# A GpSimd clear ahead of each position gather and each hop gather or scatter, and a smaller one ahead of each window gather

## The chip, the core and the metric

The kernel runs on one core of a Trainium2 chip. The metric is device microseconds of one execution, from its first to its last instruction on that core with what the device adds around it. The engines are TensorE (PE; PEld are its weight loads), VectorE (DVE), ScalarE (ACT), GpSimd (POOL) and SyncE (SP), which only issues DMAs. GpSimd issues the indirect DMAs: gathers and scatters of one row per partition, 128 rows each, whose row numbers stand in SBUF.

## The reference

Four graph layers run one after the other on 100,000 nodes of 32 features and 25,000 edges sorted by destination, each followed by a residual sum and a normalisation:

```python
x = _layernorm(x + _L0_gnn_ref(x, edge_weight, edge_attr_3, edge_index, ...), axis=-1)
x = _layernorm(x + _L1_gnn_ref(x, edge_index), axis=-1)
x = _layernorm(x + _L2_gnn_ref(x, edge_index, edge_attr_32, ...), axis=-1)
x = _layernorm(x + _L3_gnn_ref(x, edge_attr3_2x32, src, dst, ...), axis=-1)
```

- L0: each edge's weight goes through a small network (1 to 64 to 384); the result is contracted with the edge's direction and the source's features, and the messages are added up by destination.
- L1: three hops of a normalised sum over edges: `msgs = norm[:, None] * x[src]; x = segment_sum(msgs, dst)`, added up and divided by 4.
- L2: a network on both ends' features and the edge's own, then the maximum by destination.
- L3: attention over two heads: scores, a softmax by destination, messages, their sum by destination, and a last product with `W1`.

## The kernel before

A node that is no edge's destination takes a short path: its result depends on its own row alone. The kernel works with that. Edges lie in SBUF as 128 partitions of T = 196 columns; a chunk is 28 columns, so there are 7. Tables in DRAM hold one row per edge position, and an edge finds the latest value of its source there.

The stages in order of time, as the trace shows them:

1. *Histogram and positions* (to 196 us). One-hot products on PE count destinations; a table of positions, `pos_table`, is stored. POOL gathers the first source and destination rows and then, for 56 columns, each source's position (`pos_x`, named `out_short<-pos_table` in the trace; line 777). DVE meanwhile computes directions and folds weights (lines 1708 to 1760). These are many small instructions.
2. *Edge products of L0* (196 to 650 us). ACT makes the hidden layer (line 975), PE multiplies (L1310), DVE contracts. POOL gathers the other sources from `x_pos`, which needs all chunks of `x` copied and stored, then the destinations. The last 84 destination columns have a clear ahead of each gather (`gather_dst`, line 785).
3. *Hops of L1, with all nodes' short path beside them* (770 to 1204 us). POOL takes 60 columns by `short_columns` and writes them out again (lines 822 to 856), and takes and writes 22 columns by `second_columns`. Between these, PE, ACT and DVE work on 14 chunks of nodes in four lots, `nodes(...)`: PE turns rows (`n_turned`) and multiplies, ACT copies what was turned (line 1006) and takes the products, DVE normalises. The first of DVE's instructions of each half chunk is a reduction of `work`.
4. *Edge network of L2* (1243 to 1530 us). POOL gathers 7 windows of 16 columns into `work`, with a clear of `nodes_w` ahead of each gather. DVE waits for a window at line 2253 (`move_window`) and PE and ACT follow it.
5. *Attention of L3* (1530 to 1731 us and beyond). The same with windows into `A_msg`.
6. *Final scatters* (1731 to 2041 us). 196 of them, in order of readiness, line 880.

What sets the order around the change: each engine's program is written by hand, and engines meet at semaphores. POOL's queue is strictly in order. Within `gather`, `keep()` makes POOL wait for DVE now and then, so that it doesn't run too far ahead. Within `short_columns`, `keep(t)` makes it wait for a node chunk. A clear with its own semaphore `cleared`, and POOL's wait for it, stands between one indirect DMA and the next where `cleared_tile` is given: the DMA isn't begun until the clear has ended. The tile cleared is of no use at that time: `gtmp[0:HF]` is 64 by 64 words, `nodes_w` 128 partitions of 256 words.

Of the kernel before, what the change touches and what calls it, by code (L numbers as in the profile page):

```python
# [21 lines left out]
HEADS, HF = 2, 64  # L22
# [16 lines left out]
SLOTS_IN_WINDOW = 16  # L39
# [9 lines left out]
GATHER_CHUNK = 28  # L49
# [13 lines left out]
def parts_until(k):  # L63
    return sum(TABLE_PARTS[:k + 1])
# [24 lines left out]
def gnn_kernel(nc, x, src, dst, r_feat, rel, turned_attr, edge_weight, w1, b1, w2, b2,  # L89
# [12 lines left out]
    with ExitStack() as ctx:  # L102
        def sb(name, shape, dt=f32):
            return ctx.enter_context(nc.sbuf_tensor(name, shape, dt))

        def sem(name):
            return ctx.enter_context(nc.semaphore(name))
# [107 lines left out]
        gtmp = sb("gtmp", [HF + 1, HF])  # L215
# [6 lines left out]
        nodes_w = sb("nodes_w", [P, 2 * P])  # L222
# [51 lines left out]
        cleared = sem("cleared")  # L274
# [422 lines left out]
        def _(pool):  # L697
# [32 lines left out]

            node_limit, edge_limit = pool.to_reg(N_NODES - 1), pool.to_reg(E_PAD - 1)

            def gather(column, of, idx, limit, done, columns=range(T), keep=None, cleared_tile=None):

                for t in columns:
                    if keep:
                        keep()
                    if cleared_tile is not None:
                        issued["cleared"] += 1
                        pool.memset(cleared_tile, 0.0).then_inc(cleared, 1)  # L740
                        pool.wait_ge(cleared, issued["cleared"])
                    pool.indirect_dma_start(  # L742
                        out=column(t), out_offset=None, in_=of,
                        in_offset=bass.IndirectOffsetOnAxis(ap=idx[:, t:t + 1], axis=0),
                        bounds_check=limit, oob_is_err=False).then_inc(done(t), 16)
# [3 lines left out]
            issued = {"hist": 0, "radial": 0, "cleared": 0}  # L749
# [15 lines left out]
            def gather_dst(columns, keep, cleared_tile=None):  # L765
# [6 lines left out]
                   keep=keep_to_histogram)  # L772
# [2 lines left out]
            gather_dst(range(DST_FIRST * GATHER_CHUNK), keep_to_histogram)  # L775
            pool.wait_ge(pos_stored, 32)
            gather(lambda t: pos_x[:, t:t + 1], pos_table, src_i, node_limit, lambda t: pos_rows, range(plain),
                   keep=keep_to_radial)

            for k in range(XP_SLOTS):  # L780
                pool.wait_ge(x_stored[k], 16 * len(range(k, D_CHUNKS + 1, XP_SLOTS)))
# [11 lines left out]
            def short_columns(move, done, columns, keep=None):  # L793

                for t in columns:
                    if keep and keep(t):
                        pool.wait_ge(n_out, keep(t))
                    move(t).then_inc(done, 16)
                if columns.stop < FEWEST:
                    return  # L800
                turns["short"] += 1
                with pool.If(n > FEWEST):
                    for t in range(FEWEST, FEW):
                        move(t).then_inc(more_done, 16)
                    pool.wait_ge(more_done, 16 * (FEW - FEWEST) * turns["short"])
                with pool.If(n > FEW):
                    pool.wait_ge(msg_cleared, 1)
                    for t in range(FEW, T):
                        move(t).then_inc(rest_done, 16)
                    pool.wait_ge(rest_done, 16 * (T - FEW) * turns["short"])  # L810
                pool.sem_inc(short_in, 1)

            def second_columns(move):

                turns["second"] += 1
                for t in range(FEWEST2):
                    move(t).then_inc(hop_done, 16)
                with pool.If(n2 > FEWEST2):
                    for t in range(FEWEST2, T):
                        move(t).then_inc(hop_rest, 16)  # L820
                    pool.wait_ge(hop_rest, 16 * (T - FEWEST2) * turns["second"])
                pool.sem_inc(short_in, 1)
# [7 lines left out]
            def put_short(of, idx, column):  # L830
# [7 lines left out]
                          keep=lambda t: max(t - 24, 0) // 15)  # L838
# [20 lines left out]
            for k, of, order in zip((3, 4), compact, WINDOW_ORDER):  # L859

                pool.wait_ge(table_stored, 16 * parts_until(k))
                pool.wait_ge(gather_ok, k + 2)

                with pool.If(n > FEW):
                    for c in range(CHUNKS):
                        gather(lambda t: of[:, t, :], tables[k], pos_i, edge_limit, lambda t: wide_rows,
                               range(c * GATHER_CHUNK + SLOTS_IN_WINDOW, (c + 1) * GATHER_CHUNK))
                    pool.wait_ge(wide_rows, 16 * CHUNKS * (GATHER_CHUNK - SLOTS_IN_WINDOW) * (k - 2))
                pool.sem_inc(wide_in, 1)
                for i, c in enumerate(order):  # L870
                    here = window_rows[k - 3][i % SLOTS]
                    if i >= SLOTS:
                        pool.wait_ge(here, 16 * SLOTS_IN_WINDOW * (i // SLOTS))
                    gather(lambda t: of[:, t, :], tables[k], pos_i, edge_limit, lambda t: here,
                           range(c * GATHER_CHUNK, c * GATHER_CHUNK + SLOTS_IN_WINDOW), cleared_tile=nodes_w[:])

            for i, c in enumerate(LAST_ORDER):
                pool.wait_ge(final_ready, i + 1)
# [1731 lines left out]
```

## Time and profile before

| | us |
|---|---|
| three timed runs | 2048.66, 2029.43, 2053.27; median 2048.66 |
| the profiled execution's own time | 2061.06 |
| its span, first to last instruction | 2059.3 |
| busy: PE, PEld, DVE, ACT, POOL | 796.0, 595.5, 1345.8, 486.9, 1284.9 |

No engine is busy for more than two thirds of the span, so the time is made of stretches with different limits. To read it, one takes the chain of waits for the shares, then a timeline of each engine where the chain names something odd. A wait is written after the instruction that waited, as [us <-releaser]. "remote", or in the chain "another core or an unknown queue", stands where no work in the trace released it; "issue" stands where the engine waited for nothing that the trace shows. Both may be long.

### The profile page before, as it was taken

To read this page: it belongs to the slowest core of one execution; us is meant where nothing else is said; L and a number is where in the kernel's file an instruction comes from. 1 tells how busy PE (TensorE), PEld (TensorE's weight loads), DVE (VectorE), ACT (ScalarE), POOL (GpSimd) and SP (SyncE) were. 2 spreads that over 40 slices of the span, in tenths; PEclk is the share of its full clock that TensorE was granted. 3 is DMA by queue.
4 is the path that set the end of the run, shared out by engine and by line. 5 is a ranking of instruction groups with operands and counts; after the bars stand their busy time and mean duration, and the time that the engine had idled before them with its cause. 6 is when DMAs were issued, how large, how long until landed. Compare 5 with 4: busy or idle time off the path is not lost.

```text
span 2059.3 us, 14157 instructions
## 1 busy us (share of the span) xinstructions
PE 796.0 (39%) x3676; PEld 595.5 (29%) x3676; DVE 1345.8 (65%) x2600; ACT 486.9 (24%) x1014; POOL 1284.9 (62%) x1393
## 2 busy tenths in 40 slices
PE   7801545541333003616313500155621757265122
PEld 3300222220111003515313400145521657265112
DVE  9942959896958970784605496167684899397610
ACT  7721311110100121423202320033320334143200
POOL 8875576674478857515871207888128888637775
PEclk9955866786765555866756755566765776565555
DMA  8072511110110211222201412000000111010000
GB/s 313 16 240 89 201 26 29 27 30 15 20 17 12 76 43 32 100 77 87 89 6 68 158 74 98 4 8 19 18 29 12 32 28 29 18 28 22 10 12 8
DMA packets 64092, 114.25 MB, mean 55 GB/s; under 512 B 27599, under 2 KB 48648, under 8 KB 63224
## 3 DMA queue, kind: packets, MB, share of 16 engines
q1 hardware_dynamic: 24304, 80.96, 10.9%
q0 software_dynamic: 33728, 12.79, 4.5%
q10 hardware_dynamic: 5960, 19.43, 2.5%
q8 instruction: 31, 0.51, 0.1%
q14 instruction: 69, 0.57, 0.1%
HBM read 61.66 MB, written 55.21 MB: 57 GB/s over the span
## 4 chain that ended last, share of the span: by engine, by line
DVE 36%; issue 21%; POOL 20%; PE 12%; another core or an unknown queue 6%; ACT 4%; DMA 1%; DVEq 0%; ACTq 0%; POOLq 0%; PEld 0%; PEldq 0%
DVE work L1484 12%; POOL A_dst L742 8%; POOL work L742 7%; DVE work L1495 5%; PE bank L1261 4%; PE bank L1235 3%; POOL nodes_w L740 2%; POOL A_msg L742 2%; PE bank L1348 2%; DVE A_dst L1484 2%; DVE A_tmp L1484 1%; DVE r L1495 1%; DVE small L1495 1%; PE bank L1421 1%
## 5 line engine op out<-in xcount | busy, mean ns | idle before, releaser
L1495 DVE TENSOR_REDUCE work<-work 128x80 f32<-128x1280 f32 (+3 forms) x147 | 204.5, 1420 | 186.8 <-ACT work L1016 148.9
L742 POOL DMA_INDIRECT A_dst<-in_x,dst_i x196 | 223.4, 1140 | 108.7 <-DVE work L1495 48.7
L1310 PE MATMUL bank<-w2fold,work 128*128 128x384 f32 x392 | 200.6, 658 | 232.4 <-DVE work L1484 136.4
L880 POOL DMA_INDIRECT out<-A_dst,out_i x196 | 211.5, 1079 | 99.0 <-issue 61.7
L1484 DVE TENSOR_TENSOR work<-bank,work 128x384 f32<-128x384 f32 (+1 forms) x294 | 154.6, 589 | 80.3 <-remote 43.1
L1348 PE MATMUL bank<-nodes_w,small 128*128 128x128 f32 (+1 forms) x784 | 137.1, 341 | 162.0 <-ACT small L1006 95.6
L742 POOL DMA_INDIRECT A_src<-x_pos,A_tmp x140 | 145.0, 1036 | 73.1 <-issue 41.8
L1310 PEld LDWEIGHTS bank<-w2fold,work 128*128 128x128 f32 x392 | 91.0, 251 | 340.8 <-issue 310.0
L740 POOL MEMSET nodes_w<- 128x256 f32 x224 | 73.0, 326 | 168.4 <-DMA table<-A_dst 168.2
L1348 PEld LDWEIGHTS bank<-nodes_w,small 128*128 128x128 f32 (+1 forms) x784 | 125.9, 249 | 172.9 <-ACT small L1006 104.6
L742 POOL DMA_INDIRECT work<-table,pos_i x112 | 142.0, 1268 | 30.9 <-POOL nodes_w L740 30.9
L1235 PE MATMUL bank<-ident,work 128*128 128x128 f32 (+1 forms) x294 | 67.9, 346 | 235.7 <-DVE work L1484 134.8
L975 ACT ACTIVATE work<-A_tmp,b1col,w1col 65x256 f32<-65x256 f32 x98 | 58.4, 599 | 415.3 <-PE bank L1310 184.4
L742 POOL DMA_INDIRECT A_msg<-table,pos_i x112 | 132.3, 1182 | 32.2 <-POOL nodes_w L740 30.6
L1235 PEld LDWEIGHTS bank<-ident,work 128*128 128x128 f32 (+1 forms) x294 | 45.7, 185 | 240.2 <-issue 127.5
L1235 PE MATMUL bank<-ident,end_col 128*32 128x128 f32 (+2 forms) x18 | 6.8, 379 | 259.6 <-DVE end_col L1540 230.9
L831 POOL DMA_INDIRECT edge_sums<-A_sum,out_short x60 | 66.2, 1104 | 60.1 <-DVE A_sum L1484 42.2
L1235 PE MATMUL bank<-ident,A_tmp 128*65 128x128 f32 (+1 forms) x203 | 45.4, 366 | 150.6 <-DVE A_tmp L2369 144.1
L825 POOL DMA_INDIRECT A_msg<-table,nxt_i x60 | 66.5, 1108 | 55.8 <-DVE work L1484 20.2
L742 POOL DMA_INDIRECT A_src<-in_x,A_tmp x56 | 73.3, 1309 | 16.9 <-issue 16.9
L1261 PE MATMUL bank<-A_msg,A_sum 128*128 128x392 f16 x392 | 80.0, 340 | 1.7 <-ACT A_sum L929 1.7
L1421 PE MATMUL bank<-gw,A_tmp 128*128 128x128 f32 x392 | 76.7, 361 | 8.3 <-issue 5.7
(397 smaller groups left out, 2306.8 us busy)
## 6 DMA issues: line engine op xcount, KB each, us to landing
work<-in_x SPq DMA_DIRECT2D x26, 960.0 KB
x_pos<-A_sum SPq DMA_DIRECT2D x13, 990.0 KB
out<-work ACTq DMA_DIRECT2D x13, 960.0 KB
A_tmp<-ew_turned_rows ACTq DMA_DIRECT2D x49, 130.0 KB
table<-A_dst SPq DMA_DIRECT2D x2, 3136.0 KB
edge_sums<-A_dst SPq DMA_DIRECT2D x2, 3136.0 KB
table<-A_dst SPq DMA_DIRECT2D x13, 448.0 KB
A_tmp<-in_edge_attr_2x SPq DMA_DIRECT2D x49, 112.0 KB
```

The costliest lines, as they stand in the source:

```text
L740: pool.memset(cleared_tile, 0.0).then_inc(cleared, 1)
L742: pool.indirect_dma_start(out=column(t), out_offset=None, in_=of, in_offset=bass.IndirectOffsetOnAxis(ap=idx[:, t:t + 1], axis=0), bounds_ ...
L825: return lambda t: pool.indirect_dma_start(out=column(t), out_offset=None, in_=of, in_offset=bass.IndirectOffsetOnAxis(ap=idx[:, t:t + 1], ...
L831: return lambda t: pool.indirect_dma_start(out=of, out_offset=bass.IndirectOffsetOnAxis(ap=idx[:, t:t + 1], axis=0), in_=column(t), in_off ...
L880: pool.indirect_dma_start(out=out, out_offset=bass.IndirectOffsetOnAxis(ap=out_i[:, t:t + 1], axis=0), in_=A_dst[:, t, :], in_offset=None, ...
L1235: return nc.tensor.transpose(out_ap, in_ap, ident[0:n, 0:n])
L1261: last = nc.tensor.matmul(banks[6 + h][:, 0:half], lo_hot[:, 2 * slot + j, :], hi_hot[:, 2 * slot + j, h * half:(h + 1) * half], start=Fal ...
L1310: last = nc.tensor.matmul(banks[2 * (u % PAIRS_DEEP) + j][:, 0:PATHS], hid_rows[:, u % PAIRS_DEEP, j * P:(j + 1) * P], w2_rows[:], start=T ...
L1348: last = nc.tensor.matmul(node_products(i, w)[0:parts, k * P:(k + 1) * P], n_xT[:, s, k * parts:(k + 1) * parts], nodes_w[:, w * P:(w + 1) ...
L1421: last = nc.tensor.matmul(banks[2 + slot][:, j * P:(j + 1) * P], cat3_rows[:, slot, j * P:(j + 1) * P], gw2_rows[:], start=True, stop=True)
L1484: return v.tensor_tensor(out=o, in0=a, in1=b, op=op)
L1495: return v.tensor_reduce(out=o, in_=a, axis=AX, op=op)
```

## The change

The clear and its wait become a function, `pause`. It is called now in three more places: ahead of each of the 56 position gathers, ahead of each column of `short_columns` (60 gathers, 60 scatters in four pieces) and of `second_columns` (22 columns, three times). These are 242 clears of `gtmp[0:HF]` more. The 224 clears ahead of the window gathers are now of `gtmp[0:HF]` too, not of `nodes_w`. Inside the branches that these inputs don't take nothing is added.

```diff
--- before.py
+++ after.py
@@ -730,15 +730,19 @@
 
             node_limit, edge_limit = pool.to_reg(N_NODES - 1), pool.to_reg(E_PAD - 1)
 
+            def pause(tile):
+
+                issued["cleared"] += 1
+                pool.memset(tile, 0.0).then_inc(cleared, 1)
+                pool.wait_ge(cleared, issued["cleared"])
+
             def gather(column, of, idx, limit, done, columns=range(T), keep=None, cleared_tile=None):
 
                 for t in columns:
                     if keep:
                         keep()
                     if cleared_tile is not None:
-                        issued["cleared"] += 1
-                        pool.memset(cleared_tile, 0.0).then_inc(cleared, 1)
-                        pool.wait_ge(cleared, issued["cleared"])
+                        pause(cleared_tile)
                     pool.indirect_dma_start(
                         out=column(t), out_offset=None, in_=of,
                         in_offset=bass.IndirectOffsetOnAxis(ap=idx[:, t:t + 1], axis=0),
@@ -775,7 +779,7 @@
             gather_dst(range(DST_FIRST * GATHER_CHUNK), keep_to_histogram)
             pool.wait_ge(pos_stored, 32)
             gather(lambda t: pos_x[:, t:t + 1], pos_table, src_i, node_limit, lambda t: pos_rows, range(plain),
-                   keep=keep_to_radial)
+                   keep=keep_to_radial, cleared_tile=gtmp[0:HF])
 
             for k in range(XP_SLOTS):
                 pool.wait_ge(x_stored[k], 16 * len(range(k, D_CHUNKS + 1, XP_SLOTS)))
@@ -795,6 +799,7 @@
                 for t in columns:
                     if keep and keep(t):
                         pool.wait_ge(n_out, keep(t))
+                    pause(gtmp[0:HF])
                     move(t).then_inc(done, 16)
                 if columns.stop < FEWEST:
                     return
@@ -814,6 +819,7 @@
 
                 turns["second"] += 1
                 for t in range(FEWEST2):
+                    pause(gtmp[0:HF])
                     move(t).then_inc(hop_done, 16)
                 with pool.If(n2 > FEWEST2):
                     for t in range(FEWEST2, T):
@@ -872,7 +878,7 @@
                     if i >= SLOTS:
                         pool.wait_ge(here, 16 * SLOTS_IN_WINDOW * (i // SLOTS))
                     gather(lambda t: of[:, t, :], tables[k], pos_i, edge_limit, lambda t: here,
-                           range(c * GATHER_CHUNK, c * GATHER_CHUNK + SLOTS_IN_WINDOW), cleared_tile=nodes_w[:])
+                           range(c * GATHER_CHUNK, c * GATHER_CHUNK + SLOTS_IN_WINDOW), cleared_tile=gtmp[0:HF])
 
             for i, c in enumerate(LAST_ORDER):
                 pool.wait_ge(final_ready, i + 1)
```

On POOL, at the position gathers (`out_short` holds `pos_x`), before:

```order
L729 MEMSET work 128x768
L742 DMA A_src<-in_x,A_tmp 128x32 x56
L742 DMA A_dst<-in_x,dst_i 128x32 x28
L742 DMA out_short<-pos_table,A_tmp 128x1 x56
L742 DMA A_src<-x_pos,A_tmp 128x33 x140
```

and now:

```order
L729 MEMSET work 128x768
L746 DMA A_src<-in_x,A_tmp 128x32 x56
L746 DMA A_dst<-in_x,dst_i 128x32 x28
L736 MEMSET gtmp 64x64
L746 DMA out_short<-pos_table,A_tmp 128x1
```

The 56 gathers, which stood in one row, now alternate with a clear each, and the last two rows of the second piece repeat 56 times.

On POOL, at the first hop's gathers (`A_msg` from the first table), before:

```order
L790 TENSOR_LOAD n_short
L790 ISA x2
L825 DMA A_msg<-table,nxt_i 128x33 x60
L802 COMPARE_AND_BRANCH
L825 DMA A_msg<-table,nxt_i 128x33 x4
```

and now:

```order
L746 DMA A_dst<-in_x,dst_i 128x32
L794 TENSOR_LOAD n_short
L794 ISA x2
L736 MEMSET gtmp 64x64
L831 DMA A_msg<-table,nxt_i 128x33
```

Here too a clear stands ahead of each of the 60 gathers; the loads of the counts and the branches are where they were. The scatters and the later hops' gathers are changed in the same way.

On POOL, at the start of the first edge network's windows, before:

```order
L864 COMPARE_AND_BRANCH
L742 DMA work<-table,pos_i 128x32 x84
L864 UNCONDITIONAL_BRANCH
L740 MEMSET nodes_w 128x256
L742 DMA work<-table,pos_i 128x32
```

and now:

```order
L870 COMPARE_AND_BRANCH
L746 DMA work<-table,pos_i 128x32 x84
L870 UNCONDITIONAL_BRANCH
L736 MEMSET gtmp 64x64
L746 DMA work<-table,pos_i 128x32
```

The 84 gathers of the first row belong to the branch that isn't taken. Nothing moved; the clear is of a smaller tile.

## Rows read from the trace of the kernel before

**Rows 1.** The page: the span, and its section 4, the chain that ended last.
```profile
span 2059.3 us, 14157 instructions
...
DVE 36%; issue 21%; POOL 20%; PE 12%; another core or an unknown queue 6%; ACT 4%; DMA 1%; DVEq 0%; ACTq 0%; POOLq 0%; PEld 0%; PEldq 0%
```

**Rows 2.** Timeline of POOL, three places: start us, us, engine, line, operation [idle before <-releaser].
```profile
480.55 1.00 POOL L742 DMA_INDIRECT A_dst<-in_x,dst_i  x1 [0.30 <-issue]
...
677.56 0.17 POOL L740 MEMSET gtmp<- 64x64 f32 x1
678.00 1.00 POOL L742 DMA_INDIRECT A_dst<-in_x,dst_i  x1 [0.27 <-POOL gtmp L740]
...
1640.23 0.33 POOL L740 MEMSET nodes_w<- 128x256 f32 x1
1640.82 1.05 POOL L742 DMA_INDIRECT A_msg<-table,pos_i  x1 [0.27 <-POOL nodes_w L740]
```

**Rows 3.** Waits, whole span: engine line <- releaser: us in total, times, longest us.
```profile
ACT small L1006 <- remote: 121.1, 9, 31.8
```

**Rows 4.** Timeline, hops (770 to 1204 us), by engine: ACT, PE, POOL, DVE.
```profile
794.75 0.48 ACT L1006 COPY small<-bank 128x384 f32<-128x384 f32 x1 [9.43 <-remote]
...
820.82 0.48 ACT L1006 COPY small<-bank 128x384 f32<-128x384 f32 x1 [24.82 <-remote]
...
1071.72 0.48 ACT L1006 COPY small<-bank 128x384 f32<-128x384 f32 x1 [31.76 <-remote]
...
1041.98 0.85 PE L1235 MATMUL bank<-ident,work 128*128 128x128 f32 x3
...
841.40 0.99 POOL L825 DMA_INDIRECT A_msg<-table,nxt_i  x1 [20.23 <-DVE work L1484]
...
827.13 2.15 DVE L1495 TENSOR_REDUCE work<-work 128x60 f32<-128x1920 f32 x1 [50.03 <-ACT work L1016]
...
1073.00 2.15 DVE L1495 TENSOR_REDUCE work<-work 128x60 f32<-128x1920 f32 x1 [56.21 <-ACT work L1016]
```

**Rows 5.** Chain that ended last, 147 to 196 us: shares by line; start us, us, what.
```profile
by line: issue 55.6%; another core or an unknown queue 13.5%; DVE end_col L1488 8.1%; DVE end_col L1495 6.1%; DVE gw L1488 3.9%; DVE w2fold L1492 2.8%; DVE gb1c L1488 2.8%; DVE w2fold L1488 1.8%; DVE gw L1484 0.8%; DVE A_tmp L1484 0.7%; DVE
...
163.69 1.28 issue
...
172.09 1.34 issue
```

**Rows 6.** Timeline of ACT, edge products, 616 to 634 us, from POOL's clears on.
```profile
616.48 0.60 ACT L975 ACTIVATE work<-A_tmp,b1col,w1col 65x256 f32<-65x256 f32 x1 [10.60 <-remote]
...
624.95 0.60 ACT L975 ACTIVATE work<-A_tmp,b1col,w1col 65x256 f32<-65x256 f32 x1 [7.87 <-remote]
...
633.55 0.60 ACT L975 ACTIVATE work<-A_tmp,b1col,w1col 65x256 f32<-65x256 f32 x1 [3.00 <-remote]
```

**Rows 7.** Timeline of POOL: indirect DMAs that waited long for something.
```profile
209.06 0.99 POOL L742 DMA_INDIRECT out_short<-pos_table,A_tmp  x1 [16.79 <-DVE work L1495]
...
236.53 1.00 POOL L742 DMA_INDIRECT A_src<-x_pos,A_tmp  x1 [10.86 <-DMA x_pos<-A_sum]
...
538.61 0.99 POOL L742 DMA_INDIRECT A_dst<-in_x,dst_i  x1 [45.09 <-DVE work L1495]
...
962.99 1.05 POOL L825 DMA_INDIRECT A_msg<-table,idx_next  x1 [13.45 <-issue]
...
1124.16 0.98 POOL L831 DMA_INDIRECT edge_sums<-A_tmp,nxt_i  x1 [44.04 <-DVE A_tmp L1484]
```

**Rows 8.** Waits, whole span: DVE for the two edge networks' windows.
```profile
DVE work L2253 <- DMA work<-table,pos_i: 87.5, 7, 20.5
...
DVE A_msg L2253 <- DMA A_msg<-table,pos_i: 30.1, 3, 20.4
```

**Rows 9.** Timeline of DVE: the first network's fifth window, the second network's third.
```profile
1394.09 0.58 DVE L2253 COPY_PREDICATED work<-near_masks,work 128x384 f32<-128x384 uint8 x1 [3.49 <-DMA work<-table,pos_i]
...
1618.41 0.59 DVE L2253 COPY_PREDICATED A_msg<-near_masks,A_msg 128x384 f32<-128x384 uint8 x1 [2.36 <-DMA A_msg<-table,pos_i]
```

## The prediction

> **What bounds the kernel now.** I read the page's chain of waits first: DVE has 36% of it, "issue" 21%, POOL 20%, and "another core or an unknown queue" 6% [rows 1]. On one core there is no other core, so 6% of 2059.3 us, about 130 us, are waits that no work in the trace explains. The order in time then shows which engine sets the pace where. From 538 to 752 us it is POOL (row gathers); from 1243 to 1452 us POOL again (the first edge network's windows); elsewhere DVE, or DVE, ACT and PE in turn.
>
> Next, POOL's timeline for the pace of one indirect DMA. Unpaused, it takes 1.00 us and 0.30 us pass before the next: a start every 1.30 us. With a clear of 64 by 64 words ahead: 1.00 + 0.17 + 0.27 = 1.44 us. With the clear of 256 words on 128 partitions: 1.00 + 0.33 + 0.27 = 1.60 us [rows 2].
>
> Then I looked where the unexplained waits lie. All nine of ACT's in the hops are at line 1006: 121.1 us together [rows 3]. ACT waits there for PE's turned rows, which PE had finished long before (the last turn ahead of the copy at 1071.72 began at 1041.98 us), and the long waits end when POOL falls silent: the copy at 820.82 us, where POOL stops until 841.40. DVE behind them stands idle for 50.03 and 56.21 us [rows 4]. The same is seen on DVE from 147 to 196 us, beside POOL's unpaused gathers of positions: clears and additions of 0.09 to 0.29 us start some 1.4 us apart, and 69% of these 49 us (55.6% issue, 13.5% unknown), 34 us, is no work at all [rows 5]. In the window stages, with POOL at 1.60 us and PE in far more instructions, ACT's waits have not one unexplained entry. So I read these waits as a cost of POOL's unbroken stream: something the other sequencers need comes late while it lasts.
>
> Does 1.44 us suffice? Only one place shows it. PE was in such a slow stretch when POOL's small clears began at 604 us. ACT's waits behind it were 10.60, 7.87 and at last 3.00 us, with POOL never stopping [rows 6]; every other slow stretch of that loop ended in a gap of POOL's. So the stream at 1.44 us lets the others recover in about 30 us; whether it keeps a stall from starting, the trace doesn't show.
>
> **The change, part by part.**
>
> *Positions.* 56 clears, 0.14 us each: 56 x 0.14 = 7.8 us of POOL. They hide: POOL waits 16.79 us for DVE inside these gathers and 10.86 us for the stored table behind them [rows 7]. If DVE sped up, those waits would shrink, but then POOL ends at 136.5 + 56 x 1.44 = 217 us against 225.7 now, and its next consumer, DVE's third piece, comes near 313 us. Gain from the freed DVE: between 0 and 34 us. Later POOL waits 45.09 us for DVE at 538.61 [rows 7], so a gain is carried through to the POOL-bound stretch and moves it whole. I take 20, a little over half, because the one stretch at 1.44 us recovered only gradually.
>
> *Hops.* 60 gathers, 60 scatters, 44 gathers, 22 scatters: 186 clears, 26 us of POOL. Cover: POOL waits 20.23, 13.45 and 44.04 us in this stage [rows 4, 7], and nothing else waits for POOL by less than about 8 us (22 gathers end at 996, DVE asks at 1006 and they are 3 us later). Cost: 0, at worst the 26 us. Gain: ACT's nine waits would not vanish; ordinary ones at that line are 2 to 4 us, so 121.1 - 9 x 2 = 103 us is the ceiling, 0 the floor. I take 60. If all went, POOL would be next: 60 x 1.44 + 24 x 1.44 + 22 x 1.44 and so on give a last scatter near 1080 us with DVE at 1085, so the ceiling isn't cut.
>
> *Windows.* 224 clears shrink: 1.60 to 1.44 us. In the first network 112 x 0.16 = 17.9 us. DVE waits there for all seven windows, 87.5 us, the least 3.49 us [rows 8, 9]. Each window brings 2.56 us more; at the tightest, the fifth, DVE is ready at 1390.6 - 10.2 = 1380.4 and the window lands at 1394.1 - 12.8 = 1381.3, so the whole 17.9 comes through. In the second network DVE waits for the first three only (30.1 us, the third 2.36 us) [rows 8, 9]: the third window lands 7.7 us earlier, DVE is ready at 1616.05 - 5.1 = 1610.9, so 7.5 us. After it DVE is the bound, and POOL reaches its final scatters sooner than they are ready. Together 25 us. Both ends: 25 gained, or stalls that 1.60 us kept away (below).
>
> Final scatters, x_pos gathers and the first gathers are untouched, so their stalls stay, and the end of the kernel moves with the rest.
>
> Sum: 20 + 60 + 25 = 105 us. The profiled execution took 2061.06 us (span 2059.3); 2061 - 105 = 1956. The three timed runs lie 8 to 32 us below it, median 2048.66, 12 lower. Part of that spread is how the stalls fall, and fewer stalls leave less of it, so I take off 6: **1950 us**.
>
> One rule speaks against the hop and opening terms. The Trainium skill (DMA: Bandwidth & Descriptors, "Queues, rings and completion order") has each DMA engine go round between its queues packet by packet, so a busy gather queue couldn't hold up another for tens of microseconds; by it these terms are 0 and the sum is 2036. The Trainium skill (Runtime: NRT & Kernel Launch, "Instruction fetch mechanics") says sequencers stream instructions over a DMA queue in blocks of 256, mostly hidden. That would name the thing that comes late, but the 1.4 us between DVE's small instructions [rows 5] is not hidden.
>
> **Rivals.**
> 1. *The stalls stay.* 1.44 us is too near 1.30, or they have another cause (clears are only placed beside them). Then only the windows gain: 2061 - 25 = 2036, between 2015 and 2040 with the runs' offset. For it: the slow stretch went on 29 us after the clears began [rows 6]. Against: its waits fell steadily. Chance 0.2. By the skill's round-robin rule, this is the case.
> 2. *Half works*: the opening or the hops, or POOL's 26 us come into the open. 2061 - 25 - 40 = 1996, between 1985 and 2015. Chance 0.13.
> 3. *Slower: the windows begin to stall.* POOL passes 1.44 where 1.60 had kept ACT and PE clear. One episode in the hops cost 9.43 + 24.82 = 34 us [rows 4] or, at 1025 to 1087, about 60. PE issues in the windows about as much as from 236 to 1204 us, where I count eight episodes. Four at 34 us in the windows without a gain elsewhere: 2061 - 25 + 136 = 2172; with the hops cured, 2092. It needs two episodes more than the gains pay for, that is over 3 without the hops' gain. Against: if 1.44 us cures the hops, it should hold here too, with less other traffic. Chance 0.09.
> 4. The forecast: 0.58, its own range 1905 to 1985.
>
> All the change's clears are on POOL's queue in the built order, so that it doesn't do what it says is no case.
>
> Range for 8 in 10: 1905 to 2045, which leaves out rival 3 and the best tail. A change within 2% (2008 to 2090) is about what this kernel's measurement can't tell from none: rival 1 and edges, 0.2. Faster by over 2%: 0.73. Slower: 0.07.
>
> **What would show it.** Right: POOL's starts 1.44 us apart in the positions, hops and windows; ACT's unexplained waits at the line that is 1006 now down from 121 to under 60 us; DVE's small instructions of the opening well under 1 us apart; POOL's wait for DVE at the position gathers gone; windows 2.6 us closer. Wrong: waits of 10 us or more with no cause on ACT or PE inside the windows, or the hops' waits unchanged at a pace of 1.44; or POOL ending last in the hops, with DVE waiting for a gather there.

## The result, and the profile after

| | before | after |
|---|---|---|
| median, us | 2048.18 (4 runs, 2029.43 to 2053.27) | 1889.95 (4 runs, 1879.63 to 1895.93) |
| ratio | | 0.9238, 95% interval 0.9166 to 0.9309 |
| profiled execution, us (span) | 2061.06 (2059.3) | 1888.79 (1886.9) |

The change makes the kernel 158 us faster. The forecast was 1950 us, 1905 to 2045: the direction and the mechanism came, the size didn't.

The profile's page after: its span and its chain of waits:

```profile
span 1886.9 us, 14399 instructions
...
POOL 35%; DVE 28%; issue 19%; PE 10%; another core or an unknown queue 4%; ACT 2%; DMA 2%; SPq 0%; DVEq 0%; ACTq 0%; POOLq 0%; PEld 0%; PEldq 0%
```

POOL has taken DVE's place at the top [rows 1]: with fewer stalls, the engine whose pace was slowed bounds more of the time. POOL's timeline in the positions, the hops and the windows:

```profile
181.29 0.17 POOL L736 MEMSET gtmp<- 64x64 f32 x1
181.73 1.00 POOL L746 DMA_INDIRECT out_short<-pos_table,A_tmp  x1 [0.27 <-POOL gtmp L736]
...
1020.60 0.17 POOL L736 MEMSET gtmp<- 64x64 f32 x1
1021.05 0.98 POOL L837 DMA_INDIRECT edge_sums<-A_sum,out_short  x1 [0.28 <-POOL gtmp L736]
...
1280.17 0.17 POOL L736 MEMSET gtmp<- 64x64 f32 x1
1280.61 1.00 POOL L746 DMA_INDIRECT work<-table,pos_i  x1 [0.27 <-POOL gtmp L736]
```

In all three the gap between the end of one DMA and the start of the next is 0.44 to 0.45 us, for 0.30 unpaused and 0.60 with the larger clear [rows 2]. The waits of ACT and DVE after (engine, line <- releaser: us in total, times, longest):

```profile
ACT small L1012 <- remote: 7.1, 5, 3.1
...
ACT work L981 <- remote: 119.1, 16, 10.6
...
DVE work L2259 <- DMA work<-table,pos_i: 74.3, 7, 17.3
...
DVE A_msg L2259 <- DMA A_msg<-table,pos_i: 23.7, 3, 17.4
```

Line 1012 was 1006: its unexplained waits fell from 121.1 to 7.1 us [rows 3]. DVE's window waits fell by 13.2 and 6.4 us [rows 8]. The edge products, where nothing was added, still have 119.1 us of unexplained waits. DVE's first reduction of the first and the third of the four lots of nodes, and POOL where it starts the `x_pos` gathers and the later destination gathers:

```profile
769.67 2.15 DVE L1501 TENSOR_REDUCE work<-work 128x60 f32<-128x1920 f32 x1 [13.74 <-ACT work L1022]
...
969.27 2.15 DVE L1501 TENSOR_REDUCE work<-work 128x60 f32<-128x1920 f32 x1 [10.94 <-ACT work L1022]
```

```profile
219.67 1.58 POOL L746 DMA_INDIRECT A_src<-x_pos,A_tmp  x1 [0.30 <-issue]
...
520.04 0.99 POOL L746 DMA_INDIRECT A_dst<-in_x,dst_i  x1 [47.54 <-DVE work L1501]
```

The idle times of 50.03 and 56.21 us are 13.74 and 10.94 [rows 4]. Ahead of all four lots DVE stood idle for 156.2 us before (50.03, 21.36, 56.21, 28.62) and for 52.0 after (13.74, 14.89, 10.94, 12.40). POOL's wait of 16.79 us at the positions is gone and the `x_pos` gathers start 16.9 us earlier; the long wait behind them stayed, 47.54 for 45.09, so the gain was carried through, 18.6 us [rows 7]. DVE's small instructions of the opening, which the prediction wanted well under 1 us apart, are so in part only:

```profile
153.38 0.09 DVE L1740 MEMSET nodes_t<- 32x32 f32 x1 [0.37 <-issue]
154.77 0.09 DVE L1740 MEMSET nodes_t<- 32x32 f32 x1 [1.31 <-issue]
155.47 0.09 DVE L1740 MEMSET nodes_t<- 32x32 f32 x1 [0.61 <-issue]
```

Two rows where the kernel before stalled in the last stage, which the prediction hadn't looked at, and under them DVE's longest waits of the "issue" kind from 1600 to 1640 us after:

```profile
1773.72 0.42 DVE L1484 TENSOR_TENSOR work<-bank,A_tmp 128x256 f32<-128x256 f32 x1 [13.06 <-issue]
...
1794.87 0.44 DVE L2390 TENSOR_TENSOR_SCAN small<-same,small 128x28 f32<-128x28 f32 x2 [17.73 <-issue]
```

```profile
1616.15 0.44 DVE L2396 TENSOR_TENSOR_SCAN small<-same,small 128x28 f32<-128x28 f32 x2 [1.66 <-issue]
1624.59 0.42 DVE L1490 TENSOR_TENSOR work<-bank,A_tmp 128x256 f32<-128x256 f32 x1 [1.31 <-issue]
```

By four of POOL's starts in the two traces (first hop gather 770.73 and 749.76, first window gather 1243.55 and 1118.55, first final scatter 1731.33 and 1575.13, end) the 172.4 us of span divide so: up to the hops 21.0, hops 104.0, windows 31.2, last stage 16.2. The 104.0 of the hops are what DVE's idle times above lost, 104.2. The last two are to be read with care: POOL starts its first final scatter 1.3 us after its last window gather, waiting for nobody, while DVE still has two windows to come. So that start tells where POOL is, not where the network is.

### The profile page after: what moved, and what is told of

Read it like the earlier page. It is cut to its first block, busy times and chain, and to the rows that moved or that the text cites. A ratio compares the mean times of both kernels' runs of the same rounds, so it can differ in the third digit from the quotient of the medians.

```text
span 1886.9 us, 14399 instructions
## 1 busy us (share of the span) xinstructions
PE 768.2 (41%) x3676; PEld 571.8 (30%) x3676; DVE 1345.4 (71%) x2600; ACT 486.4 (26%) x1014; POOL 1327.8 (70%) x1635
## 4 chain that ended last, share of the span: by engine, by line
POOL 35%; DVE 28%; issue 19%; PE 10%; another core or an unknown queue 4%; ACT 2%; DMA 2%; SPq 0%; DVEq 0%; ACTq 0%; POOLq 0%; PEld 0%; PEldq 0%
POOL A_dst L746 8%; DVE work L1490 8%; POOL work L746 8%; POOL A_msg L831 7%; POOL edge_sums L837 5%; PE bank L1267 4%; POOL gtmp L736 4%; POOL A_msg L746 3%; DVE work L1501 3%; DVE A_dst L1490 2%; PE bank L1241 2%; DVE A_tmp L1490 1%; DVE r L1501 1%; PE bank L1450 1%
## 5 line engine op out<-in xcount | busy, mean ns | idle before, releaser
L886 POOL DMA_INDIRECT out<-A_dst,out_i x196 | 217.8, 1111 | 77.2 <-issue 61.8
L736 POOL MEMSET gtmp<- 64x64 f32 x550 | 91.7, 167 | 142.6 <-DMA table<-A_dst 109.4
L1241 PE MATMUL bank<-ident,work 128*128 128x128 f32 (+1 forms) x294 | 62.9, 325 | 219.6 <-DVE work L1490 123.4
L1354 PE MATMUL bank<-nodes_w,small 128*128 128x128 f32 (+1 forms) x784 | 122.1, 315 | 62.5 <-ACT small L1012 56.3
L1354 PEld LDWEIGHTS bank<-nodes_w,small 128*128 128x128 f32 (+1 forms) x784 | 111.6, 224 | 72.3 <-ACT small L1012 64.7
L1241 PEld LDWEIGHTS bank<-ident,work 128*128 128x128 f32 (+1 forms) x294 | 41.8, 172 | 224.0 <-issue 120.7
L831 POOL DMA_INDIRECT A_msg<-table,nxt_i x60 | 75.0, 1250 | 17.9 <-POOL gtmp L736 9.3
L746 POOL DMA_INDIRECT A_src<-in_x,A_tmp x56 | 73.3, 1309 | 16.9 <-issue 16.9
L837 POOL DMA_INDIRECT edge_sums<-A_sum,out_short x60 | 72.2, 1204 | 17.6 <-POOL gtmp L736 11.9
```

Of the source, the lines that this page charges most:

```text
L736: pool.memset(tile, 0.0).then_inc(cleared, 1)
L746: pool.indirect_dma_start(out=column(t), out_offset=None, in_=of, in_offset=bass.IndirectOffsetOnAxis(ap=idx[:, t:t + 1], axis=0), bounds_ ...
L831: return lambda t: pool.indirect_dma_start(out=column(t), out_offset=None, in_=of, in_offset=bass.IndirectOffsetOnAxis(ap=idx[:, t:t + 1], ...
L837: return lambda t: pool.indirect_dma_start(out=of, out_offset=bass.IndirectOffsetOnAxis(ap=idx[:, t:t + 1], axis=0), in_=column(t), in_off ...
L886: pool.indirect_dma_start(out=out, out_offset=bass.IndirectOffsetOnAxis(ap=out_i[:, t:t + 1], axis=0), in_=A_dst[:, t, :], in_offset=None, ...
L1241: return nc.tensor.transpose(out_ap, in_ap, ident[0:n, 0:n])
```

## The experiments

**The theory:** where POOL issues indirect DMAs without a pause, the other engines' instructions come late. **Its rivals:** the stalls fall where they like and the clears are only beside them; they are tied to a place in PE's program; or what helps isn't the gap between two DMAs but POOL's clear, or its wait for it. The experiments ran on four chips, and this proved to matter more than anything else. The first three chips served for one session each, the fourth for two with the same time of the kernel before; so what is said here of a chip could also be of its session. "Hop stage" is the time from the first hop gather to the first window gather.

### Each part alone, on a chip without stalls

```diff
 e1: pause() in short_columns and second_columns alone
 e2: cleared_tile=gtmp[0:HF] at the position gathers alone
 e3: windows with cleared_tile=gtmp[0:HF], not nodes_w[:], alone
 e4: the whole change, and clears at x_pos, the other 84 destination gathers, final scatters
```

> The change in the hops alone: 186 clears of 64 by 64 words, positions unpaused, windows with the large clear as before. Theory A (the clear opens the stream of indirect DMAs, and PE and ACT get through): ACT's unexplained waits at its hop copies fall from 121 us to about 10, and the kernel gains what the two traces show between DVE's first sum of the nodes and the first window, 100 us: 2048 to about 1945. Theory B (the hops gained because the positions and DVE's weight folding moved them against each other): under 30 us of gain, 2020 or more. If the gain of the last stage, some 25 us, belongs to the hops by chance of alignment, it would be 1920.

> The change at the 56 position gathers alone. Theory A: DVE's small instructions between 147 and 196 us come closer, POOL's release at 538.61 us comes 19 us earlier, and nothing else moves: 2048 to about 2029. Theory B: the hops and the last stage gain from this shift too: under 2000.

> The smaller clear ahead of the 224 window gathers alone. Theory A: 17 us in the first network, 7 us in the second, and no unexplained wait inside either: 2048 to 2024. If the last stage's 25 us come from POOL beginning its scatters earlier against DVE: about 2000. The slower rival (windows stall at 1.44 us) has to show over 2048.

> The changed kernel with a clear also ahead of the 140 gathers from x_pos, the other 84 destination gathers and the 196 final scatters; only the first 84 gathers stay unpaused. Theory A: DVE's unexplained waits of the edge products (63.5 us) mostly go, the PE chain behind the last scatters too; POOL's pace of 1.44 us costs 0.14 x 84 in the stretch where POOL alone sets the pace, 12 us, and 0.16 x 85 = 13.6 us at the end. Net gain of 20 to 50 us on 1890: about 1855. If the pace at 1.44 us alone is what costs, without stalls to save: 1915.

Measured, where before took 1799.0 us (13 runs): hops 1825.25, ratio 1.012 (1.007 to 1.017); positions 1808.68, 1.0039 (1.0021 to 1.0056); windows 1773.44, 0.983 (0.9788 to 0.9873); the change with the further clears of e4 1867.88, 1.0359 (1.0318 to 1.04). The same program that took 2048 us takes 1799 here. The chain of the kernel with the hops' clears alone has no "another core or an unknown queue":

```profile
POOL 56%; DVE 20%; issue 16%; PE 4%; ACT 1%; DMA 1%; POOLq 0%; DVEq 0%; SPq 0%
```

None of these four traces has a single "remote" wait. So the stalls are not the kernel's alone, but the kernel's on certain chips. Where they don't occur, clears that are added only cost: 186 of them in the hops, 0.14 us each, 26 us, the price that the prediction had as "at worst". My expectations of the first two kernels, made for a chip with stalls, didn't come. The whole change wasn't run on this chip; its three parts add up to 1809 us, 0.6% more than before.

### The kernels as they are, none of the clears, and PE's program moved

```diff
 c3: before, without any cleared_tile (84 destination gathers, 224 window gathers)
 e10: before, ahead of the edge products on PE
+            for _ in range(40):
+                turn(banks[7][:, P:2 * P], ident[:], P)
```

> The kernel before, unchanged, profiled once more. Two chips have shown it so far: in the case's own runs 2048 us, with waits on ACT, DVE and PE that nothing in the trace explains (121.1 us of them at ACT's line 1006); on the chip of my first four experiments 1799 us and not one such wait. If the stalls belong to the kernel and only their fall is chance, a profile should show some of them again, with a time between 1799 and 2048. If they belong to the chip that it runs on: on the chip of the first experiments 1799 us within 5 and no wait of this kind over 1 us; on another chip either that or 2048.

> The whole change, unchanged. Where there are no stalls, only two things are left of it: the added clears on POOL's path and the smaller clears in the windows. The three parts alone gave +26.3 us (hops), +9.7 us (positions) and -25.6 us (windows) against 1799.0; if they add, 1809 us, ratio 1.006. If the change has a gain that needs all three parts together, under 1790. Where the stalls are there, 1890 against 2048 as in the result.

> The kernel before without any of its clears: neither the 84 of 64 by 64 words ahead of gathers of destination rows nor the 224 of 256 words ahead of the windows' gathers. Without stalls POOL's pace alone decides: 84 x 0.14 = 12 us ahead of the hops, of which what POOL bounds comes through, and in the windows 112 x 0.30 = 34 us for the first network, where the change's 112 x 0.16 = 18 us and a few for the second network gave 25.6. So 1799 - 25.6 x 30/16 = 1751, less up to 12: 1740 to 1755. By the theory that an unbroken stream of gathers stalls the others, the windows would stall here: over 1799, up to 1935 if four episodes of 34 us fall there.

> The kernel before with 40 more turns of 128 by 128 on PE, into a bank that is free there, ahead of the edge products; nothing reads them. They move every later PE instruction 80 places on in its program. If a stall is tied to a place in PE's program (its instructions come late there), the stalls of the edge products, which stood at about 1090, 1210, 1325 and 1560 PE records before and after the change, stand 80 records later counted with the added ones: the same work is done earlier. If it is tied to the work or to the time, they stay with the work. Where there are no stalls: about 40 x 0.07 = 3 us more at most, 1799 to 1802.

On a second chip: before 2040.09 us (19 runs), the same kernel once more 2050.1 (ratio 1.0017, 0.9961 to 1.0073), the changed one 1890.14 (0.9268, 0.9219 to 0.9318), without clears 2160.62 (1.059, 1.0514 to 1.0665), with PE's padding 2040.81 (1.0031, 0.9979 to 1.0083). The result is reproduced, and taking the clears away costs 120 us though POOL is then faster. In that trace the stalls go on where before has its small clears, from 604 us [rows 6]:

```profile
632.55 0.60 ACT L975 ACTIVATE work<-A_tmp,b1col,w1col 65x256 f32<-65x256 f32 x1 [9.90 <-remote]
643.75 0.60 ACT L975 ACTIVATE work<-A_tmp,b1col,w1col 65x256 f32<-65x256 f32 x1 [10.60 <-remote]
654.95 0.60 ACT L975 ACTIVATE work<-A_tmp,b1col,w1col 65x256 f32<-65x256 f32 x1 [10.60 <-remote]
666.15 0.60 ACT L975 ACTIVATE work<-A_tmp,b1col,w1col 65x256 f32<-65x256 f32 x1 [10.60 <-remote]
```

The rival of chance placement is out. So is PE's program: with 80 more records on PE ahead, the stalls of the edge products began with the same work at about the same time as without. First the kernel with the padding, then before on the same chip; the first row of each is ACT's instruction for the 29th of 98 pairs of columns:

```profile
286.95 0.60 ACT L975 ACTIVATE work<-A_tmp,b1col,w1col 65x256 f32<-65x256 f32 x1 [9.93 <-issue]
297.45 0.60 ACT L975 ACTIVATE work<-A_tmp,b1col,w1col 65x256 f32<-65x256 f32 x1 [9.90 <-remote]
307.99 0.60 ACT L975 ACTIVATE work<-A_tmp,b1col,w1col 65x256 f32<-65x256 f32 x1 [9.94 <-remote]
```

```profile
285.98 0.60 ACT L975 ACTIVATE work<-A_tmp,b1col,w1col 65x256 f32<-65x256 f32 x1 [9.93 <-PE bank L1310]
297.17 0.60 ACT L975 ACTIVATE work<-A_tmp,b1col,w1col 65x256 f32<-65x256 f32 x1 [10.59 <-remote]
307.67 0.60 ACT L975 ACTIVATE work<-A_tmp,b1col,w1col 65x256 f32<-65x256 f32 x1 [9.90 <-remote]
```

PE makes eight records at line 1310 for one pair of columns, so a stall tied to a place on PE would have come ten pairs sooner. It comes with the same pair, and at the later stalls with the same or the next one.

The two kernels on one chip give the cleanest division, 150.3 us of span: up to the first hop gather 17.5 (770.34 to 752.80), hop stage 100.6 (471.0 to 370.4), windows 30.4, last stage 1.8.

### Without one part, and without the wait for the clear

```diff
 e11: the change without pause() in short_columns and second_columns
 e7: the change with no cleared_tile in the windows
 e6: the change, and pause(gtmp[0:HF]) ahead of each final scatter
 e9, in pause():
+                pool.wait_ge(cleared, issued["cleared"])
                 issued["cleared"] += 1
                 pool.memset(tile, 0.0).then_inc(cleared, 1)
-                pool.wait_ge(cleared, issued["cleared"])
```

> The changed kernel without the clears ahead of the hops' gathers and scatters; those of the positions and the smaller ones of the windows stay. Where the stalls are there: by the milestones of the two traces the hops gave 103 us, so 1890 + 103 = 1993; by my forecast's term 1890 + 60 = 1950; if the hops' gain came from the earlier stages alone, 1890. ACT's waits behind PE's turns in the hops should be back at 115 to 130 us. Where no stalls are: the clears in the hops cost 26 us alone, so 26 less than the changed kernel there (1809 by the sum of the parts): 1783.

> The changed kernel with no clear at all ahead of the windows' gathers. Where the stalls are there: the kernel without any clears lost 72 us of DVE's and ACT's time in the second network's windows, so the same stalls should come here. POOL gains 112 x 0.14 = 16 us in the first network; if two or three stalls of 20 to 45 us fall in the second, 1890 - 16 + 80 = 1954, between 1920 and 2010. If one clear anywhere else is enough, 1870 to 1875. Where no stalls are: 16 us and a few less than the changed kernel there, 1809 - 23 = 1786.

> The changed kernel with a 64 by 64 clear ahead of each of the 196 final scatters too. Where the stalls are there: from 1984 to 2041 us of the kernel before, PE's weight loads and turns start 1.40 us apart beside scatters at 1.29 us, and the last stage after the change still has such a stretch. If the clear lets PE go on there, it gains up to 10 us in the last 60 us, less what POOL's 0.14 x 196 = 27 us cost where POOL is the one that is late: 1880 to 1917. Its sign tells which is more. Where no stalls are, the clears only cost: 1809 + up to 27.

> The changed kernel, but POOL does not wait for a clear before it issues the DMA behind it; it waits only for the one before that. The clears stay, 0.17 us each; the 0.27 us of idle behind each shrinks, so the pace should lie between 1.30 and 1.44 us. Where the stalls are there: if it is POOL's idle moment that lets the others go on, the hops' waits come back in part or whole, 1950 to 2030; if it is the clear itself (work of POOL that is no DMA), the time stays at 1890 or falls by what POOL's pace gives in the windows, 112 x up to 0.14 = up to 16 us: 1874 to 1890. Where no stalls are: up to 25 us less than the changed kernel.

On a third chip, before 2040.15 us (7 runs): without the hops' clears 1984.52, ratio 0.9741 (0.9647 to 0.9834); with the windows unpaused 1949.2, 1957.22, 2004.31 and 2009.05, too scattered for an interval; with the final scatters' clears 1891.84, 0.9277 (0.9214 to 0.9341); with clears that aren't waited for 2072.45, 1.0148 (1.0078 to 1.0217). The hops' part is worth about 96 us (0.9741 less 0.9268, of 2040; the two ratios come from two chips, and their intervals leave some 20 us either way), not 60: ACT's unexplained waits there are back at 133.8 us, the hop stage at 463.8. The windows needed their clears too, since even the fastest of those four runs is 59 us above the changed kernel's 1890; unpaused, the second network stalls on DVE and ACT:

```profile
1472.09 0.43 DVE L1490 TENSOR_TENSOR work<-bank,A_tmp 128x256 f32<-128x256 f32 x1 [47.47 <-issue]
```

The unwaited clear is the sharpest result: all clears are there, POOL does the same work, and all of the gain is gone. Its POOL timeline in the hops:

```profile
1059.41 0.98 POOL L837 DMA_INDIRECT edge_sums<-A_sum,out_short  x1 [0.16 <-issue]
1060.38 0.17 POOL L737 MEMSET gtmp<- 64x64 f32 x1
1060.72 0.98 POOL L837 DMA_INDIRECT edge_sums<-A_sum,out_short  x1 [0.16 <-issue]
```

The gap is 0.33 us, hardly more than the 0.30 of no clear. As each DMA takes 1.00 us whatever stands ahead of it, no run tells a longer gap from a slower pace of DMAs; "gap" below stands for either.

### The gap or the wait; the other parts; the edge products too

```diff
 e12, in pause():
-                pool.memset(tile, 0.0).then_inc(cleared, 1)
+                pool.memset(tile[:, 0:1], 0.0).then_inc(cleared, 1)
 e13: the change without the positions' clears
 e14: the change with cleared_tile=nodes_w[:] in the windows
 e5: the change, and cleared_tile=gtmp[0:HF] at x_pos and the other 84 destination gathers
 e8: the change, pause() twice ahead of each move of the hops
 e16: as e5, and pause() ahead of the first 76 final scatters
```

> The changed kernel with every clear cut from 64 by 64 words to one word on 64 partitions, still waited for. It should take about 0.06 us in place of 0.17, so the DMAs start about 1.33 us apart in place of 1.44. The kernel whose clears were not waited for had the same pace, 1.33 us, and every stall: 2072 us. Two readings of that are told apart. If the gap between one DMA and the next is what the others need (0.30 and 0.33 us stall, 0.44 does not), the stalls come back: 2040 to 2080. If it is that POOL waits for its own clear, whatever the gap, they stay away and POOL's pace gives up to 16 us in the windows: 1870 to 1890. Where no stalls are: 10 to 20 us less than the changed kernel there.

> The changed kernel without the 56 clears at the position gathers. Where the stalls are there: my forecast's term, and the milestones of the two traces, say 20 us: 1910. If the opening's stalls only move into POOL's next wait, 1890. DVE's small instructions of 160 to 175 us should start 1.40 us apart again. Where no stalls are: 7 to 10 us less than the changed kernel there.

> The changed kernel, but with the windows' clears of 256 words on 128 partitions as before. By the forecast's term and the milestones, the smaller clears gave 24 us ahead of the last stage, and the same edit alone gave 25.6 us where no stalls are. So 1890 + 25 = 1915. If they also caused the 25 us of the last stage, which I had not forecast, up to 1940.

> The changed kernel with clears also ahead of the 140 gathers of x_pos and the 84 of destination rows that had none. There the changed kernel still stalls (ACT's waits at the line of the Fourier features, 119 us, 16 of them; DVE's 63 us). From the first x_pos gather to the last of the destination rows it takes 511 us; with clears there, and no stalls on the chip, 482; without either 451. If the clears cure these stalls too: 1890 - 29 = 1861. If POOL's pace is the bound there whatever the stalls, 224 x 0.14 = 31 us more: 1921.

> The changed kernel with two clears, each waited for, ahead of each of the hops' 186 moves; the gap between two DMAs there is then about 0.88 us in place of 0.44. The gaps seen so far in the hops and ACT's unexplained waits at the line of the hops' copies: 0.30 us 121 (before), 0.33 us 133, 0.38 us 71, 0.44 us 7 to 22. By a gap that has to be long enough, these waits are 0 to 5 us now. POOL needs 186 x 0.44 = 82 us more; where POOL is the bound in the hops that comes through: one clear cost 18 us from the first hop gather to the first window where no stalls are, so the second costs at least as much, up to 82: 1908 to 1972. If the last 10 us of stalls had been on the path and POOL had cover, 1880.

> The changed kernel with clears also ahead of the 140 gathers of x_pos, the 84 of destination rows that had none, and the first 76 of the 196 final scatters (three of eight groups). With the edges' clears alone 1865; there the last stage still had ACT's unexplained waits of 6 to 11 us from 1582 to 1629 us, beside the first scatters, and took 310 us from the first scatter to the last, where a run without such waits took 285. All 196 clears cured these waits, and took as much of POOL's time: 309. If 76 clears cure them for 76 x 0.14 = 11 us of POOL: 1865 - 25 + 11 = 1851. If POOL's time counts from the start there, 1865 + 11 = 1876. Where no stalls are on the chip: 1799 + 26 + 10 - 26 + up to 31 + 11, about 1850.

On a fourth chip, before 2060.27 us for the first four and 2062.69 for the last two (7 runs each). Small clears, waited for: 1917.76, ratio 0.9289 (0.9151 to 0.9426). Neither reading was right as I put it: the small clear takes 0.11 to 0.12 us and the gap is 0.39:

```profile
1059.52 0.98 POOL L837 DMA_INDIRECT edge_sums<-A_sum,out_short  x1 [0.28 <-POOL gtmp L736]
1060.49 0.12 POOL L736 MEMSET gtmp<- 64x1 f32 x1
1060.89 0.98 POOL L837 DMA_INDIRECT edge_sums<-A_sum,out_short  x1 [0.28 <-issue]
```

and ACT's unexplained waits in the hops are between the two:

```profile
ACT small L1012 <- remote: 70.8, 15, 7.3
```

Had the wait alone been what helps, they would be as after the change. With two clears (gap 0.64 us, not the 0.88 that I expected: they run back to back) there is none left, but POOL pays: 1922.66, 0.9323 (0.9287 to 0.9358). Together, on the chips that stall:

| gap between two DMAs in the hops, us | kernels | ACT's unexplained waits there, us | hop stage, us |
|---|---|---|---|
| 0.30 | before (two traces), no clears, change without the hops | 121.1, 116.6, 133.1, 133.8 | 464 to 473 |
| 0.33 | clears not waited for | 132.8 | 464.4 |
| 0.39 | small clears | 70.8 | 398.0 |
| 0.44 | the change (two traces), six kernels more | 7.1 to 21.8 | 366 to 374 |
| 0.64 | two clears | 0 | 402.5 |

Without stalls on the chip the hop stage takes 345.8 us unpaused and 364.0 with clears. So the change's clears take away nearly all of the stall, at 18 us of POOL's pace; a longer gap only costs. The least that does it isn't the same everywhere: with small clears the stretch from the first window gather to the end takes 755.5 us, where it takes 764.6 and 768.4 in the changed kernel's two traces. Small clears in the windows with the full ones in the hops weren't run.

Without the positions' clears 1919.5, 0.9334 (0.9228 to 0.9439). The changed kernel itself wasn't run on this chip; by its 0.9268 elsewhere it would take 1909, so the positions give about 10 us, with an uncertainty of some 20. By the first hop gather, 768.55 us here, it is 10.1 and 19.3 us against two kernels of this chip that are the changed one up to there (two clears 758.47, windows as before 749.21). Windows as before: 1945.77, no interval (1918.43 to 1949.92), 9 to 41 us above that 1909, so the time can't say whether it is more than the 25 expected. Its trace can: from the first window gather to DVE's third window of the second network it takes 380.1 us, against 353.0 in the kernel without the positions' clears, 27.1 more. The rest are stalls of 14.40 and 17.14 us in the last stage, which fall in some traces of any of these kernels.

With clears in the edge products too: 1864.65 us, 0.9089 (0.9007 to 0.9171), the 1861 expected: the stage takes 483.3 us there for 511.3, and ACT has no unexplained wait at line 981. The first final scatters' clears add nothing to it, 1866.52, 0.9059 (0.9018 to 0.91). These two beat the changed kernel where there are stalls; where there are none, the smaller window clears alone, 1773.44, are best of what ran.

## Why the prediction was right or wrong

- *The mechanism* was right: the unexplained waits are a cost of POOL's unbroken stream. That it holds on three of four chips only couldn't be seen in one trace.
- *Does 1.44 us suffice?* Yes, nearly: 7.1 us of 121.1 are left. It is close to the edge: at a gap of 0.39 more than half is back.
- *Positions:* 20 us forecast, 18.6 carried through, 17.5, 10.1 and 19.3 by the other traces. Right, with DVE's stalls in the opening only part cured.
- *Hops, the step that failed:* "I take 60", between 0 and a ceiling of 103. The ceiling came: 104.0 and 100.6 us by the two pairs of traces, about 96 by the kernel without this part. The middle was taken without a reason of its own: the one partial recovery [rows 6] was a stall that had already begun, and says nothing of how many begin. A middle does exist, 70.8 us of waits at a gap of 0.39; that 0.44 lies past it no row of before could show. With 103 the forecast would have been 1907.
- *Windows:* 25 forecast, and right. From the first window gather to DVE's third window of the second network, the last that DVE waits for, it takes 22.7 us less in the first pair of traces, 26.2 in the second, and 27.1 on the fourth chip; the time fell by 25.6 us where there are no stalls. The 31.2 and 30.4 above have POOL's own lead in them. From its third to its seventh window DVE gained 1.0 us in the second pair (161.1 to 160.1): after the third it is the bound, as forecast.
- *The last stage,* "untouched, so their stalls stay": in the profiled pair DVE goes from the third to the seventh window in 162.6 us, for 189.7 before, a gain of 27.1 that nothing in the sum had. It isn't the change's. The second pair has 1.0, and on the fourth chip four traces of kernels with clears in the hops are as long, 183.3 to 190.6. For one of these, the one with clears in the edge products, the profiled execution took 1889.93 us and the other four 1862.28 to 1866.44: the stall falls in some executions, with the change as without it. The execution that I summed against had fallen on the long side, by 28.6 us against the other trace of before. With the hops at 103 the sum is 2061 - 20 - 103 - 25 = 1913; this stall covers the 24 from there to 1889.
- *Rival 3,* stalls begin in the windows: they didn't at a gap of 0.44, but do at 0.30, where the second network lost 47.47 us in one wait. *Rival 1,* and the rule that DMA engines go round between queues packet by packet (the Trainium skill, DMA: Bandwidth & Descriptors, "Queues, rings and completion order"): by it these terms were to be nothing, but a change of 0.14 us in POOL's gap moved 100 us in the hops. So either another thing than a DMA queue is what comes late, or the rule doesn't bound it; no run tells which.
- *POOL's 26 us* in the hops, priced at nothing, cost 26 us where there are no stalls, 18 of them in the hop stage; on the other chips the gain hid them.

## What to carry to other kernels

Where an engine shows waits that no work explains, beside a long run of indirect DMAs, give that run a short pause (here 0.44 us between two in place of 0.30), and look for the least that does it: in the hops 0.33 did nothing, and 0.64 cost more than it gave. Such a pause is an insurance: on the chip without stalls it only costs, so time both kernels on more than one chip before you keep it. When a cure has a threshold that no row shows, forecast the ceiling and nothing as two cases with their chances; the half of the ceiling is a case of its own, and wants a reason of its own. And sum against more than one trace of the kernel before: here one execution held a stall of 28.6 us that another didn't.

## What the runs showed of the hardware

- The same program took 1799.0 us on one chip and 2040 to 2063 on three, with no unexplained wait in the one's traces and, in the first trace of before, some 280 us of them on ACT alone.
- In a stall, an engine starts one instruction about every 1.40 us in the stretches read here (0.70 at places, as from 154.77 to 155.47 us after the change), be it a clear of 0.09 us or a weight load of 0.18. DVE in the opening, then PE's weight loads beside the last scatters (every second instruction, so 2.8 us), both of before:

```profile
170.60 0.09 DVE L1734 MEMSET nodes_t<- 32x32 f32 x1 [2.46 <-issue]
172.00 0.09 DVE L1734 MEMSET nodes_t<- 32x32 f32 x1 [1.32 <-issue]
173.43 0.09 DVE L1734 MEMSET nodes_t<- 32x32 f32 x1 [1.34 <-issue]
```

```profile
1987.54 0.18 PEld L1235 LDWEIGHTS bank<-ident,A_msg 128*128 128x128 f32 x1 [2.70 <-issue]
1990.33 0.18 PEld L1235 LDWEIGHTS bank<-ident,A_msg 128*128 128x128 f32 x1 [2.61 <-issue]
1993.13 0.18 PEld L1235 LDWEIGHTS bank<-ident,A_msg 128*128 128x128 f32 x1 [2.62 <-issue]
```

- That it is the supply of instructions that comes late is only a guess. The Trainium skill (Runtime: NRT & Kernel Launch, "Instruction fetch mechanics") has instructions fetched over DMA in blocks of 16 KiB, 256 instructions each; the trace of before agrees on the first of its two instruction queues, 31 packets of 16384 bytes. The two queues, by the page of the profile of before:

```profile
q8 instruction: 31, 0.51, 0.1%
q14 instruction: 69, 0.57, 0.1%
```

- Against the guess: none of these packets took more than 1.36 us, and on the chip without stalls the longest (in the windows-only kernel) took 1.47, so none was slow by itself; and by that section late blocks would make one wait in 256 instructions, and not one at each (an argument, not a run). Whether the packets were asked for late the trace doesn't show. PE's own place in its program was ruled out for the edge products, ACT's and DVE's were not tried. So what it is that comes late stays open, and why three chips show it and one doesn't.
